# Two exponential groups of an attention step moved from ScalarE to VectorE, and the query weights loaded ahead of x

## The reference, cut to what matters

```python
Q, K, V = X @ Wq + bq, X @ Wk + bk, X @ Wv + bv          # 16 heads of 16
scores = einsum('bhqd,bhkd->bhqk', q, k) / sqrt(16)      # 16 x 2048 x 2048
attn   = softmax(scores)
x = layernorm(X + einsum('bhqk,bhkd->bhqd', attn, v) @ Wo + bo)   # in a layout of (d, head)
x = layernorm(x + down(silu(gate(x)) * up(x)))           # 256 -> 1024 -> 256
```

## Time and profile before

| | |
|---|---|
| runs | 643.88 to 647.7 us, median 645.85 |
| the profiled execution | 647.61 us, its span 645.6 us |
| granted TensorE clock, mean of the span | 0.985 |
| TensorE busy | 621.8 us (96%) |
| ScalarE busy | 532.7 us (83%) |
| VectorE busy | 152.6 us (24%) |
| an ordinary step | 29.33 us |
| a norm step | 31.99 us |

### The profile page before, as it was taken

The page is one execution under the profiler, slowest core; times in us unless marked ns, Lnnn a source line. Parts: engine busy times, 40 slices in busy tenths (PEclk is TensorE's granted clock), DMA queues, the critical chain, the costliest instruction groups (busy, mean ns, idle before and its releaser), DMA issues.

```text
span 645.6 us, 9666 instructions
## 1 busy us (share of the span) xinstructions
PE 621.8 (96%) x3952; PEld 260.0 (40%) x3952; DVE 152.6 (24%) x280; ACT 532.7 (83%) x613; POOL 47.7 (7%) x47
## 2 busy tenths in 40 slices
PE   6997999999999999999999999999999999979994
PEld 5883222222222323222232322223322226958873
DVE  5672000000001201000012200001411005695684
ACT  3635999999999899999999999999899996233351
POOL 5616000000000000000000000000300000010001
PEclk8996999999999999999999999999999999999998
DMA  9565982211102010101110111111010000110111
GB/s 195 105 102 72 126 118 45 33 18 25 25 11 61 9 27 10 29 6 31 44 29 9 27 21 16 27 33 40 8 28 8 7 4 9 36 34 2 32 34 33
DMA packets 36051, 24.67 MB, mean 38 GB/s; under 512 B 24802, under 2 KB 30818, under 8 KB 35410
## 3 DMA queue, kind: packets, MB, share of 16 engines
q1 hardware_dynamic: 34580, 23.22, 21.5%
q10 hardware_dynamic: 1424, 0.79, 0.5%
HBM read 6.56 MB, written 4.33 MB: 17 GB/s over the span
## 4 chain that ended last, share of the span: by engine, by line
PE 90%; DVE 6%; ACT 1%; DMA 1%; issue 1%; ACTq 0%; DVEq 0%
PE ps L1058 39%; PE ps L1042 32%; PE ps L917 5%; PE ps L1154 5%; PE ps L1133 5%; PE ps L1082 2%; DMA w_raw<-in_L_attn_Wq 1%; DVE h L826 1%; DVE h_lo L814 1%; ACT probs L559 1%; DVE stats L790 1%; PE ps L1096 1%; DVE out_tmp L807 1%; PE ps L903 0%; DVE r_tmp L786 0%
## 5 line engine op out<-in xcount | busy, mean ns | idle before, releaser
L559 ACT ACTIVATE probs<-ps 128x1024 f32<-128x1024 f32 x512 | 470.3, 1410 | 24.0 <-PE ps L1042 24.0
L1058 PE MATMUL ps<-probs,v_all 128*17 128x512 f32 x2048 | 271.0, 601 | 0.5 <-ACT probs L559 0.4
L1042 PE MATMUL ps<-q_slot,k_stack 51*128 51x512 f32 x1024 | 228.9, 492 | 3.6 <-DVE q_slot L669 3.0
L1042 PEld LDWEIGHTS ps<-q_slot,k_stack 51*128 51x128 f32 x1024 | 94.0, 185 | 264.2 <-ACT probs L559 245.7
L708 DVE COPY attn_q<-ps 128x512 f32<-128x512 f32 x16 | 11.1, 692 | 371.9 <-PE ps L1058 371.9
L578 ACT ACTIVATE sg<-ps,sgate_c 128x512 f32<-128x512 f32 x32 | 22.0, 689 | 53.5 <-PE ps L1154 53.5
L1058 PEld LDWEIGHTS ps<-probs,v_all 128*17 128x17 f32 x2048 | 34.0, 95 | 68.9 <-issue 62.3
L476 POOL TENSOR_TENSOR rstd<-var_eps,minus_half 128x4 f32<-128x4 f32 x4 | 4.1, 1022 | 497.8 <-DVE var_eps L740 497.8
L1154 PE MATMUL ps<-qy,wg 128*128 128x512 f32 x128 | 36.0, 403 | 4.9 <-DVE h L826 4.9
L1154 PE MATMUL ps<-qy,wu 128*128 128x512 f32 x128 | 34.4, 391 | 0.0
L1133 PE MATMUL ps<-wd,h_lo 128*128 128x256 f32 x128 | 30.9, 283 | 0.0
(11 more groups left out here) (88 smaller groups left out, 272.7 us busy)
## 6 DMA issues: line engine op xcount, KB each, us to landing
q_slot<-qy SPq DMA_DIRECT2D x64, 64.0 KB
k_stack<-k_part SPq DMA_DIRECT2D x12, 256.0 KB
at_dram<-attn_q SPq DMA_DIRECT2D x64, 34.0 KB
at<-at_dram SPq DMA_DIRECT2D x8, 272.0 KB, 3.0
q_slot<-qy SPq DMA_DIRECT2D x64, 32.0 KB
x_tok<-in_L_attn_X SPq DMA_DIRECT2D x14, 128.0 KB, 7.1
k_stack<-k_part SPq DMA_DIRECT2D x12, 128.0 KB
out<-out_tmp SPq DMA_DIRECT2D x12, 128.0 KB, 2.2
```

The costliest lines, as they stand in the source:

```text
L559: nc.scalar.activation(probs[:, u % 3, 2 * p:2 * p + 2, :].rearrange("p a b -> p (a b)"), ps[:, 2 * ring:2 * ring + 2, :].rearrange("p a b ...
L1042: last = nc.tensor.matmul(ps[:, 2 * ring + half, :], k_stack[s % QUADS][base:base + ROWS, p, kt * P:(kt + 1) * P], q_slot[slot][base:base ...
L1058: last = nc.tensor.matmul(ps[32 * hh:32 * hh + VW, ACC, :], v_all[:, kt, NQ * (s % QUADS) + hh, :], probs[:, u % 3, hh, :], start=(kt == 0 ...
```

## The change

1. **Exponentials on VectorE.** From step 2 on, the group of heads 0 and 1 (`g` even) of two key tiles in a step goes to VectorE: tiles 3 and 9 in ordinary steps, 4 and 10 in turn steps, and only tile 10 in norm steps (`poly_tiles`). That makes 8 x 2 + 3 x 2 + 3 x 1 = 25 of the 512 groups. `exponentials(n)` takes eight operations of 128 x 1024: one that reads PSUM and writes the exponent and fraction as bits of an int32, two bit operations in SBUF, and five scalar_tensor_tensor steps of the polynomial. Each but the fourth waits for the one in front of it.
2. **Order.** The ring place of such a group is free when the first operation has read it (`poly_read`). Its value product comes later than its turn: tile 3 at place 8, 4 at 9, 9 at 14, 10 at 15 (`value_order`); the other tiles of heads 0 and 1 move up. Heads 2 and 3 keep their order.
3. **ScalarE** goes through the 487 other groups, writes into six half buffers instead of three whole ones, and adds a constant (`log_factor`) to the exponent, so that both kinds of exponential carry the same factor, which the softmax takes out.
4. **VectorE's program** has `save_attn(s - 1)` at the start of step `s` with the exponentials behind it; in norm steps the one exponential group stands behind the whole normalization, in turn steps the second `ln1_parts` stands between the two groups.
5. `turn_y` moves from tiles 4 and 7 to tiles 1 and 6. The cast of `wd` waits for the last polynomial, whose buffers lie in its place, and TensorE waits for it only ahead of the first down product.
6. **Start.** On ScalarE's DMA queue `Wq` stands ahead of the two pieces of x.

```diff
+        def poly_tiles(s):
+            if s < 2:
+                return []
+            if s > QUADS and s % QUADS == 1:
+                return [10]
+            if s > QUADS and s % QUADS == 2:
+                return [4, 10]
+            return [3, 9]
+        def value_order(s):
+            behind = {3: 8, 4: 9, 9: 14, 10: 15}
+            late = {behind[kt]: kt for kt in poly_tiles(s)}
+            others = [kt for kt in range(UPS) if kt not in poly_tiles(s)]
+            return [late[i] if i in late else others.pop(0) for i in range(UPS)]
...
+            act.dma_start(w_raw[:, 0, :].rearrange("p (k n) -> p k n", k=KO),
+                          Wq.rearrange("(k p) n -> p k n", p=P)).then_inc(w_loaded[0], 16)
             for d in range(2, CH):
                 act.dma_start(x_tok[UW * d:UW * (d + 1), 0:TPC, :], x_view[0, d]).then_inc(x_loaded[0], 16)
-            act.dma_start(w_raw[:, 0, :].rearrange("p (k n) -> p k n", k=KO),
-                          Wq.rearrange("(k p) n -> p k n", p=P)).then_inc(w_loaded[0], 16)
...
-            for g in range(2 * UPS * STEPS):
+            for n, g in enumerate(BY_ACT):
                 act.wait_ge(scores_ready, g + 1)
+                if n >= HALVES and products_of(BY_ACT[n - HALVES]) > waited:
+                    waited = products_of(BY_ACT[n - HALVES])
+                    act.wait_ge(pv_done, waited)
...
+            def exponentials(n):
+                g = BY_POLY[n]
+                ring, res = g % 3, poly[n % 2]
+                mant_f, bits_f = mant.bitcast(f32), bits.bitcast(f32)
+                if n:
+                    dve.wait_ge(poly_done, n)
+                dve.wait_ge(scores_ready, g + 1)
+                nc.vector.tensor_scalar(bits[:], ps[:, 2 * ring:2 * ring + 2, :], TO_BITS, LOWEST, ALU.mult, ALU.max
+                                        ).then_inc(poly_read, 1)
+                dve.wait_ge(poly_read, n + 1)
+                nc.vector.tensor_scalar(mant[:], bits[:], FRACTION, ONE, ALU.bitwise_and, ALU.bitwise_or
+                                        ).then_inc(poly_bits, 1)
+                dve.wait_ge(poly_bits, n + 1)
+                nc.vector.tensor_scalar(bits[:], bits[:], EXPONENT, BIAS, ALU.bitwise_and, ALU.bitwise_xor
+                                        ).then_inc(poly_exponent, 1)
+                if n >= 2:
+                    dve.wait_ge(pv_done, products_of(BY_POLY[n - 2]))
+                nc.vector.scalar_tensor_tensor(res[:], mant_f[:], MONIC[4], mant_f[:], ALU.add, ALU.mult
+                                               ).then_inc(poly_step, 1)
+                for i in (3, 2, 1):
+                    dve.wait_ge(poly_step, 4 * n + 4 - i)
+                    nc.vector.scalar_tensor_tensor(res[:], res[:], MONIC[i], mant_f[:], ALU.add, ALU.mult
+                                                   ).then_inc(poly_step, 1)
+                dve.wait_ge(poly_exponent, n + 1)
+                dve.wait_ge(poly_step, 4 * n + 4)
+                nc.vector.scalar_tensor_tensor(res[:], res[:], MONIC[0], bits_f[:], ALU.add, ALU.mult
+                                               ).then_inc(poly_done, 1)
...
+                for i, kt in enumerate(poly_tiles(s)):
+                    exponentials(POLY_NO[2 * (UPS * s + kt)])
+                    if parts and i == 0:
+                        ln1_parts(c, 1)
...
+                elif g - 3 in POLY_NO:
+                    pe.wait_ge(poly_read, POLY_NO[g - 3] + 1)
                 else:
-                    pe.wait_ge(exp_done, g - 2)
+                    pe.wait_ge(exp_done, ACT_NO[g - 3] + 1)
...
-                if c >= 0 and s % QUADS == 2 and kt in (4, 7):
-                    turn_y(c, kt // 7)
+                if c >= 0 and s % QUADS == 2 and kt in (1, 6):
+                    turn_y(c, kt // 6)
```

More of the change, by code:

```diff
@@ L93, in layer_program @@
         warm = place("warm", [P, TPC], f32)
+        log_factor = place("log_factor", [P, 1], f32)
         minus_half = place("minus_half", [P, TPC], f32)
@@ L107, in layer_program @@
         out_tmp = place("out_tmp", [P, TPC, HID], f32, at_parts + 28 * KB)
+        bits = place("bits", [P, 2, CW], i32, at_parts + 16 * KB)
+        mant = place("mant", [P, 2, CW], i32, at_parts + 20 * KB)
+        poly = [place(f"poly{i}", [P, 2, CW], f32, at_parts + 24 * KB + 4 * KB * i) for i in range(2)]
         at = region(32 * KB)
@@ L259, in keys_of, with products_of @@
             return 16 * 2 * NQ * 2 if quad == 0 else 16 * (2 * NQ + 2)
+        def poly_tiles(s):
[11 more added lines that the diff above has]
+            return [late[i] if i in late else others.pop(0) for i in range(UPS)]
+        ORDER = [value_order(s) for s in range(STEPS)]
+        BY_POLY = [2 * (UPS * s + kt) for s in range(STEPS) for kt in poly_tiles(s)]
+        POLY_NO = {g: n for n, g in enumerate(BY_POLY)}
+        BY_ACT = [g for g in range(2 * UPS * STEPS) if g not in POLY_NO]
+        ACT_NO = {g: n for n, g in enumerate(BY_ACT)}
+        def products_of(g):
+            s, kt = g // 2 // UPS, g // 2 % UPS
+            return UPS * s + (kt if g % 2 else ORDER[s].index(kt)) + 1
         def part_of(c, k, part):
@@ L486, in _ @@
             nc.gpsimd.tensor_copy(wu[:], up8[:].bitcast(i8)).then_inc(ffn_w_ready, 1)
-            for quad in range(2, QUADS):
-                pool.wait_ge(k_loaded[quad], keys_of(quad))
+            pool.wait_ge(poly_done, len(BY_POLY))
             nc.gpsimd.tensor_copy(wd[:], down8[:].bitcast(i8)).then_inc(ffn_w_ready, 1)
@@ L605, in then @@
                 dve.wait_ge(dve_step, steps[0])
+            nc.vector.memset(log_factor[:], math.log(EXP_FACTOR)).then_inc(factor_ready, 1)
             nc.vector.memset(shift[:].bitcast(i32), 0).then_inc(zero_ready, 1)
@@ L758, in ln1_parts @@
                                         ).then_inc(yt_ready, 1)
+            def exponentials(n):
+                g = BY_POLY[n]
+                ring, res = g % 3, poly[n % 2]
+                mant_f, bits_f = mant.bitcast(f32), bits.bitcast(f32)
+                if n == 0:
+                    for quad in range(2, QUADS):
+                        dve.wait_ge(k_loaded[quad], keys_of(quad))
+                if n:
[21 more added lines that the diff above has]
+                                               ).then_inc(poly_done, 1)
             dve.wait_ge(bo_added, TT // 2)
             for s in range(STEPS):
-                save_attn(s)
                 c = s // QUADS - 1
-                if s >= QUADS and s % QUADS == 0:
+                if s:
+                    save_attn(s - 1)
+                norm = c >= 0 and s % QUADS == 1
+                parts = c >= 0 and s % QUADS == 2
+                if norm:
                     scale_attn(c)
@@ L1055, in prob_times_v @@
                     pe.wait_ge(attn_saved, s)
-                pe.wait_ge(exp_done, 2 * (u + 1))
-                for hh in range(NQ):
+                tiles = [ORDER[s][kt], kt]
+                pairs = [2 * (UPS * s + tiles[p]) + p for p in range(2)]
+                pe.wait_ge(exp_done, 1 + max(ACT_NO[g] for g in pairs if g in ACT_NO))
+                if pairs[0] in POLY_NO:
+                    pe.wait_ge(poly_done, POLY_NO[pairs[0]] + 1)
+                for hh in range(NQ):
+                    g = pairs[hh // 2]
+                    if g in POLY_NO:
+                        prob = poly[POLY_NO[g] % 2][:, hh % 2, :]
+                    else:
+                        prob = probs[:, ACT_NO[g] % HALVES, hh % 2, :]
                     last = nc.tensor.matmul(ps[32 * hh:32 * hh + VW, ACC, :],
-                                            v_all[:, kt, NQ * (s % QUADS) + hh, :],
-                                            probs[:, u % 3, hh, :], start=(kt == 0), stop=(kt == TT - 1))
+                                            v_all[:, tiles[hh // 2], NQ * (s % QUADS) + hh, :],
+                                            prob, start=(kt == 0), stop=(kt == TT - 1))
                 last.then_inc(pv_done, 1)
```

33 lines of the change are left out of this document (24 added, 9 removed).

## The result

The changed kernel takes 670.76 us (median of 4 runs, 668.92 to 672.83) against 645.6 us before (4 runs), a ratio of 1.0384 with a 95% interval of 1.0348 to 1.042. It is 25 us slower; the forecast was 8 us faster, and no rival had this cause. The profiled execution has a span of 666.9 us against 645.6; it is the shortest of the four, and the one profiled before was among the longest, so the two traces show 21 of the 25 us.

What follows compares the result with a forecast made beforehand. ScalarE's exponentials were taken to bound attention, TensorE 10% behind; −10.2 (ordinary), −3.2 (turn), +1.8 and +3.6 (norm steps) gave −8.0 us, a forecast of 638 us, range 630.5 to 645.

Steps and rivals of the forecast that it cites:

- Six half buffers, log_factor, the later value order: 0: ScalarE's new buffers and added constant, and the reordered value products: no new wait, so 0 us.
- ordinary step with two skips: Eight attention steps, two groups each leaving ScalarE: −1.27 us per step, together −10.2 us.
- turn step: Three attention steps with two skips and a transpose: −1.07 us each, together −3.2 us.
- norm steps 5 and 9, late read: VectorE reads tile 10's scores only after the normalization, so ScalarE waits: +0.9 us each, together +1.8 us.
- norm step 13, casts in the way: VectorE's normalization is slowed beside GpSimd's casts, so the ring waits for its read: +3.6 us.
- chain on VectorE: Eight operations per exponential group take 9.3 us, from 9.0 to 10.4, short enough for ring and value product.
- start, `Wq` first: Query weights load before two pieces of x; the first product stays at 11.23 us: 0, ±1.5 us.
- `wd` late: Later cast of `wd` after the last polynomial: 0 us, at most 1.96 if uncovered.
- A: Rival: VectorE's chain is too long, 11.9 us, nothing gained from about 11.0; slower, 655.5 us; chance 0.08.
- B: Rival: VectorE's bit operations run at one element a cycle, chain 10.4 us; 641 us; chance 0.25.
- C: Rival: the ring loses nothing at a skip, so more of the 22.9 us arrives; 631 us; chance 0.12.
- D: Rival: TensorE is at its limit in fact, so nothing moves; 646 to 650 us; chance 0.10.

Runs made afterwards that it cites:

- a_imm: The changed kernel with the exponential's added constant as a number in the instruction again, not an operand of one value per partition; 637.4 us, ratio 0.9872.
- b_ptr: The kernel before with the exponential adding an operand of one value per partition that holds zero; 687.69 us, ratio 1.0644.
- b_wq: The kernel before with only the query weights moved ahead of x on ScalarE's DMA queue; 643.19 us, ratio 0.9958.
- dose2: The changed kernel with the constant as a number, no VectorE group in norm steps, and one polynomial step done three times; 644.47 us, ratio 1.0000.
- casts_late: As a_imm, but GpSimd's casts of the gate and up weights wait for the end of step 13's scores; 633.0 us, ratio 0.9808.

## Why the prediction was wrong

**The step that failed is "Six half buffers, log_factor, the later value order: 0".** `log_factor` costs 0.088 us on each exponential of the engine that sets the pace. Over 487 of them that is 43 us, of which 33 reached the end (670.8 to 637.4). The rest was lost where something else was waited for anyway. Between a_imm and the changed kernel an ordinary step grows by 2.29 us instead of 2.64 (30 exponentials), since the waits behind its skips (0.17 and 0.18 us) are gone; steps 5 and 9 grow by 1.5 instead of 2.7, step 13, which VectorE's late read holds up, by 0.1. The forecast looked for a new wait in this edit and found none. It didn't ask what the instruction itself takes in its new form, and the trace of before had the answer. From its page, part 5, and the line view of ScalarE:

```profile
L540 ACT ACTIVATE qy<-ps,bq_c 128x512 fp32r<-128x512 f32 x8 | 5.5, 690 | 4.0 <-PE ps L917 4.0
L571 ACT CAST h_hi<-h 128x512 fp32r<-128x512 f32 x32 | 19.6, 613 | 2.7 <-DVE h L826 2.7
L527 ACT CAST xt_hi<-ps 128x512 fp32r<-128x512 f32 x8 | 4.3, 588 | 0.0
```

For the same 512 elements, 690 ns with an operand `bq_c` and 588 to 613 in casts without one. The Trainium skill, page ScalarE: Activation LUTs, states it outright, in the paragraph on ACTIVATE under What ACT_TABLE_LOAD costs: each operand of one value per partition adds about 93 ns. The runs agree: 88 ns in a stream of 1024 columns (1.002 − 0.914). Weighed against the diff, the Trainium skill's figure gives an estimate of 487 x 0.093 = 45 us, so −8 + 45 = +37 for the change: the right side, and too much by the part that waits swallow. With the measured 0.088 the sum is −8 + 43 = +35.

Point by point, with a_imm as the kernel in which that step is taken out:

| step of the prediction | forecast | found |
|---|---|---|
| ScalarE sets the pace, TensorE 10% behind | 0.917 a group | right; b_ptr moves the time by 42 us through ScalarE alone |
| ordinary step with two skips | 28.07 us | 28.06 |
| turn step | 28.3 | 28.3 |
| norm steps 5 and 9, late read | 32.8 (+0.9) | 32.6 and 32.5 (+0.6, +0.5) |
| norm step 13, casts in the way | 35.5 (+3.6) | 38.2 (+6.2); the read 3.1 late instead of 2.7, about 2.6 for the lower clock |
| chain on VectorE | 9.3, bounds 9.0 to 10.4 | 8.9 |
| start, `Wq` first | 0, ±1.5 | −2.7, and −1.3 at equal granted clock |
| `wd` late | 0 | the end part unchanged within 0.1 us |
| log_factor | 0 | +33 us |

**The chain** came out just under its lower bound, by a slip of the same kind turned round. The 0.749 us of the scalar_tensor_tensor belongs to one that has an operand `sup_c`; the two-tensor instruction of the same size takes 0.69. The polynomial's constants are numbers in the instruction, and it was measured at 1.22, not 1.28. That `sup_c` makes the difference is an inference: no row has this instruction at 512 elements without it. The clue to the failed step stood in a row that the forecast used. Of the bit operations' two bounds the 0.74 was the near one.

**The start** went by "the queue carries the same bytes, so its last piece lands about when `Wq` did", and so by a first product at 11.23. In b_wq's profile the last piece lands at 7.98 us where `Wq` landed at 9.56, and the first product still stands at 11.24. The time came out 2.7 us shorter, outside the ±1.5, and 1.3 at equal clock, inside it; why it is shorter stays open.

**The rivals.** A's mechanism is real: dose2 shows it, with the gain gone at a chain of about 11.4 us, where 11.0 was computed for the kernel with the norm steps' loss (the same sum without that loss gives 11.5); the changed kernel is at 8.9 and not subject to it. B is out (0.69 us). C is out: a skip costs what the ring says. D is out, since ordinary steps fell by 1.27 us. The true case, an instruction on the bounding engine that grows by a tenth, was not among them, though it needs no wait, no queue and no neighbour. In the chances two entries don't fit the text: the 0.12 for "within" needs all of D's 0.10, not half of it, and the range up to 645 leaves out all of D (646 to 650), not its upper part. Neither bears on the failure.

With these sizes a_imm comes out. From the first save to the last it takes 524.98 − 84.36 = 440.6 us where the kernel before takes 534.84 − 88.32 = 446.5, so −5.9, and the forecast's −8.0 with the norm steps as found (+7.3 for +5.4) is −6.1. With the start's −2.7 that is −8.6 us, and the medians differ by 8.3. Left open is where the start's gain comes from, and how much of it is owed to the order of the loads and how much to the clock: the first exponential varies by some 2 to 3 us between profiles, and no run was made on that alone.

## What to carry to other kernels

On the engine that sets the pace, price the form of each instruction that a diff touches, not only the waits around it: here an operand in place of a number made each exponential follow 0.088 us later, nearly a tenth, and turned a gain into a loss, and the trace had both forms side by side. When work is moved off that engine, check in each stage when the receiving engine can begin and when the result is due, and leave out the stages where it starts late, since a ring place that is not read stops everyone. A chain that fits between its start and its due time is free, and worth nothing more when shortened; its slack can be computed from the rows to some tenths of a microsecond.

## What the runs showed of the hardware that was not expected

- Exponentials of 128 x 1024 with an operand of one value per partition follow each other at 1.002 us in step 1 and 1.004 later, with a number at 0.914 and 0.917. On VectorE the scalar_tensor_tensor of 512 elements takes 749 ns with such an operand; that of 1024 takes 1219 to 1225 with a number, no more than the two-tensor operation.
- Bit operations with two numbers on int32 in SBUF take 694 ns for 1024 elements, against 1223 for the same kind of instruction that reads PSUM.
- In a_imm the clock fell to 0.50 (1.2 GHz) towards the end of an idle time of TensorE of 4.11 us and came back about 6.3 us after TensorE had begun again; in the changed kernel, behind an idle time of 3.90 us, it was at 0.50 for 3.4 us. Idle times of 1.1 us and less in steps 5 and 9 had no such stretch behind them. In a_imm ScalarE's wait of 3.9 us was followed by 2.6 us more.
- Each of VectorE's scalings that met a cast on GpSimd ended only after it: four take 4.50 us beside two casts of 1.9, 6.08 beside three, and 1.38 beside none, in step 5 and in step 13 of casts_late. A scaling beside a cast takes 1.96 to 1.98 us, one alone 0.40.
